# Two exchanges in TensorE's order within an attention visit: a q/k turn with the output product, the turn of x with a q/k product

## The chip, the cores and the metric

One core of a Trainium2 chip runs the whole program. The metric is the device time of one execution in microseconds. A kernel is executed several times and the median is given; one further execution is profiled.

## The reference, cut to what matters

Four blocks run one after the other on 16 sequences of 256 tokens with 128 channels. The change is in the last of them, a network of six layers, each an attention and then a feed-forward part:

```python
def attn_layer(x, Wqkv, qs, ksc, Wo):        # 16 heads of 64, x is 256 x 128 per sequence
    q, k, v = jnp.split(x @ Wqkv, 3, -1)
    q = l2norm(q) * qs;  k = l2norm(k) * ksc
    q = q * cos * scale + rotate_half(q) * sin * scale
    k = k * cos / scale + rotate_half(k) * sin / scale
    out = local_attention(q, k, v)           # windows of 32 look at themselves and the one before
    return out @ Wo                          # added to x
```

(Condensed: the reshapes to heads and the shift of half the channels by one token are left out.)

## The kernel before, in words

All activations stay on the chip. In `l1_network` the five engines each have a program of their own, held together by semaphores; each engine works through its program strictly in the written order. A layer has a prologue, 16 attention visits (one for a sequence, written `attention(N, u, b, prev, nxt, nxt2)`, with N the running number of the sequence and u its parity), and the feed-forward part. `prev`, `nxt` and `nxt2` say whether there is a sequence before, after, and two after this one in the layer.

A visit is a software pipeline over two halves j = 0, 1 (128 tokens each). In a half, TensorE works on three sequences: it finishes N - 1 (or the first half of N), scores N, and prepares N + 1. Its program, L2112 to L2169, in the order of a half:

1. masks into the score banks (L2046), then the attention products of the half before, `weigh` (L2083, 128 small matmuls);
2. two q/k products of N + 1 (`project_qk`, L2008) and two v products (L2015); each is one matmul of 128 x 512 that runs in two passes;
3. the scores (L2058, 128 small matmuls);
4. two output turns (`turn_output`, L2031, four transposes of 128 x 128 each), which ScalarE copies (L2285);
5. the output product (`output`, L2038, eight matmuls in two passes each), which VectorE adds to X (L2454);
6. four q/k turns (`turn_qk`, L2024, four transposes each; numbers 4 to 7 of N in half 0, 0 to 3 of N + 1 in half 1), which ScalarE copies (L2279). They read what GpSimd normed (L1927). Between the first and the second stand the turns of the attention weights (`turn_weights`, L2070, eight transposes), between the second and the third a third q/k product;
7. in half 1, if there is a sequence two after, the turn of its x (`turn_x`, L2001, two transposes), which ScalarE copies in two parts (L2253, L2254) for the products of the next visit;
8. the fourth q/k product, whose square ScalarE takes (L2259) before VectorE rotates it (L2410).

The PSUM banks set a second order. The q/k products have banks 0 and 1 in turn. All of v products, output turns, output product ("y"), q/k turns and the turn of x share banks 2 and 3, which alternate in the order of the list `SHARED` (L1660). Each use waits until the use two before it, which had the same bank, has been read:

```python
for use in SHARED:
    if there[use[2]]:
        out[use] = (2 + at % 2, before[-2])
        before.append(use)
        at += 1
```

`freed` (L1985) turns the kind of that earlier use into a wait: for a turn or an output turn it is ScalarE's copy, for y it is VectorE's addition. The order of ScalarE is a list of its own (L2312 to L2349): in each half the squares, the inverse norms, the copies of v, the two copies of output turns, two exponentials, the copy of the first q/k turn, two copies of turned weights, the copy of the second, a square, the copies of the third and fourth, a square; at the end of half 1 the copy of x. VectorE's order in a half (L2419 ff., `attention`) is: the output's norm, two rotations, a sum of squares, the maxima, a sum of squares, the addition of y (L2454), the sums of exponentials (L2436) and their reciprocals, two more rotations.

Of the kernel before, what the change touches and what calls it, by code (L numbers as in the profile page):

```python
# [80 lines left out]
def held(eng, passed):  # L81

    eng.sem_inc(passed, 1)
# [1554 lines left out]
def l1_network(nc, env, weights, consts):  # L1638
# [16 lines left out]
    def place(c):  # L1655

        return c // 4, 1 - c // 2 % 2, c % 2


    SHARED = ([("v", 0, 1), ("v", 1, 1), ("o", 2, -1), ("o", 3, -1), ("y", 0, -1)] + [("turn", 4 + r, 0) for r in range(4)]  # L1660
              + [("v", 2, 1), ("v", 3, 1), ("o", 0, 0), ("o", 1, 0), ("y", 1, -1)]
              + [("turn", r, 1) for r in range(4)] + [("x", 0, 2)])

    def banks(u, prev, nxt, nxt2):

        there = {-1: prev, 0: True, 1: nxt, 2: nxt2}
        before = [("turn", 3, 0), ("x", 0, 1)] if nxt else [("turn", 2, 0), ("turn", 3, 0)]
        at = u if nxt else 0
        out = {}
# [5 lines that stand above are left out]
        if not nxt:  # L1675
            for use in (("y", 0, 0), ("o", 2, 0), ("o", 3, 0), ("y", 1, 0)):
# [3 lines that stand above are left out]
        return out  # L1680
# [7 lines left out]
    with ExitStack() as ctx:  # L1688
# [121 lines left out]
        def after(eng, s, value):  # L1810

            eng.wait_ge(s, value + START)
# [171 lines left out]
        def _(pe):  # L1984
            def freed(kind, c, N):  # L1985

                if kind == "x":
                    after(pe, s_xT, N + 1)
                elif kind == "v":
                    after(pe, s_V, 4 * N + c + 1)  # L1990
                elif kind == "turn":
                    after(pe, s_qkT, 8 * N + c + 1)
                elif kind == "o":
                    after(pe, s_OT, 4 * N + c + 1)
                elif kind == "y":
                    after(pe, s_x, 2 * N + c + 1)
# [7 lines left out]
            def project_qk(N, c):  # L2004
                j, t, half = place(c)
                after(pe, s_t, 8 * N + c - 1)
                after(pe, s_xT, N + 1)
                nc.tensor.matmul(pp[:, c % 2, :], xT[:, j * P:(j + 1) * P],  # L2008
                                 wqkv[:, t * I + 512 * half:t * I + 512 * half + 512],
                                 start=True, stop=True).then_inc(s_qk, 1)  # L2010
# [8 lines left out]
            def turn_qk(N, r, bank):  # L2019
                j, t, half = place(r)  # L2020
                after(pe, s_kn, 8 * N + r + 1)
                for g in range(4):
                    o = 512 * half + g * P
                    last = nc.tensor.transpose(pp[:, bank, g * P:(g + 1) * P], pre[:, j, t, o:o + P], ident[:, :])  # L2024
                last.then_inc(s_turn, 1)
# [9 lines left out]
            def output(N, j, bank):  # L2035
                after(pe, s_OT, 4 * N + 2 * j + 2)
                for k in range(I // P):
                    last = nc.tensor.matmul(pp[:, bank, 0:C], OT[:, j, k % 2, k // 2, :],  # L2038
                                            wo[:, k, :], start=(k == 0), stop=(k == I // P - 1))
                last.then_inc(s_y, 1)  # L2040

            def masks(N, j):

                after(pe, s_sub, 4 * N + 2 * j)
                for e in range(2):
                    nc.tensor.matmul(pS[:, e, :].rearrange("p (i s) -> p i s", s=2 * W), eye[:, :],  # L2046
                                     bcast(win[:, j, :], 1, 8), start=True, stop=False, skip_group_check=True)
# [17 lines left out]
            def turn_weights(N, j):  # L2065
                for e in range(2):
                    after(pe, s_On, 4 * N + 2 * j)
                    after(pe, s_E, 4 * N + 2 * j + e + 1)
                    for c in range(4):
                        last = nc.tensor.transpose(pW[:, e, c * P:(c + 1) * P], E[:, e, c * P:(c + 1) * P],  # L2070
                                                   ident[:, :])
                    last.then_inc(s_ETp, 1)

            def weigh(u, j):
                for c in range(4):
                    for e in range(2):
                        for w in range(NW):
                            m = (NW * j + w) // 2
                            v = V if w % 2 else Vx
                            o = c * P + e * D  # L2080
                            for f in range(2):
                                r = D * f
                                last = nc.tensor.matmul(pW[W * w:W * w + W, f, o:o + D],  # L2083
                                                        ET[r:r + D, e, c, W * w:W * w + W],
                                                        v[r:r + D, u, m, o:o + D], start=True, stop=True)
                                if c == 3 and e == 1 and w == NW - 1:
                                    last.then_inc(s_PV, 1)

            def weights_ready(pair, N, u, j):
                after(pe, s_ET, 4 * N + 2 * j + 2)  # L2090
                if j == 0:
                    after(pe, s_vx[u], 288 * (pair + 1))
# [19 lines left out]
            def attention(N, u, b, prev, nxt, nxt2):  # L2112
                at = banks(u, prev, nxt, nxt2)

                def bank(*use):
                    kind, c, d = at[use][1]
                    freed(kind, c, N + d)
                    return at[use][0]

                for j in range(2):  # L2120
                    if j == 1:
                        weights_ready(pairs[0], N, u, 0)
                    elif prev:
                        weights_ready(pairs[0], N - 1, 1 - u, 1)
                    if not nxt:
                        after(pe, s_qkT, 8 * N + 4 * j + 4)
                    masks(N, j)
                    if j == 1:
                        weigh(u, 0)
                    elif prev:  # L2130
                        weigh(1 - u, 1)
                    if nxt:
                        project_qk(N + 1, 4 * j)
                        project_qk(N + 1, 4 * j + 1)
                        after(pe, s_qkT, 8 * N + 4 * j + 4)
                        project_v(N + 1, 2 * j, bank("v", 2 * j, 1))
                        project_v(N + 1, 2 * j + 1, bank("v", 2 * j + 1, 1))
                    scores(j)
                    if j == 1:
                        turn_output(N, 0, bank("o", 0, 0))  # L2140
                        turn_output(N, 1, bank("o", 1, 0))
                    elif prev:
                        turn_output(N - 1, 2, bank("o", 2, -1))
                        turn_output(N - 1, 3, bank("o", 3, -1))
                    if prev:
                        output(N - 1, j, bank("y", j, -1))
                    d = j
                    if nxt or not d:
                        turn_qk(N + d, 4 - 4 * j, bank("turn", 4 - 4 * j, d))
                    turn_weights(N, j)  # L2150
                    if nxt or not d:
                        turn_qk(N + d, 5 - 4 * j, bank("turn", 5 - 4 * j, d))
                    if nxt:
                        project_qk(N + 1, 4 * j + 2)
                    if nxt or not d:
                        turn_qk(N + d, 6 - 4 * j, bank("turn", 6 - 4 * j, d))
                        turn_qk(N + d, 7 - 4 * j, bank("turn", 7 - 4 * j, d))
                    if j == 1 and nxt2:
                        turn_x(N + 2, u, bank("x", 0, 2))
                    if nxt:  # L2160
                        project_qk(N + 1, 4 * j + 3)
                if not nxt:
                    weights_ready(pairs[0], N, u, 1)
                    held(pe, s_held)
                    weigh(u, 1)
                    output(N, 0, bank("y", 0, 0))
                    turn_output(N, 2, bank("o", 2, 0))
                    turn_output(N, 3, bank("o", 3, 0))
                    output(N, 1, bank("y", 1, 0))  # L2169
# [527 lines left out]
```

## Time and profile before

| | |
|---|---|
| median of 3 runs | 4761.02 us (4757.34 to 4762.45) |
| profiled execution, its own time | 4745.73 us |
| span of its profile, first to last instruction | 4743.8 us |
| TensorE matmuls busy | 4145.6 us (87%) |
| VectorE, ScalarE, GpSimd busy | 3378.1 us (71%), 2449.9 us (52%), 2175.5 us (46%) |
| mean granted clock of TensorE | 0.957 |

The span is what lies between the first and the last instruction of the profiled execution; the 1.9 us around it belong to the same execution. The busy times are sums over the whole program, of which the six layers are the stretch from about 1,100 us on. In the rows, PE is TensorE's matmul, PEld its load of weights, ACT ScalarE, DVE VectorE, POOL GpSimd; `n_pp<-ident,n_pre` is what is written and what is read. A "x8" behind a row is the number of instructions that it merges.

### The profile page before, as it was taken

Reading aid. Unit: us, or ns where it says so; the run is one execution under the profiler, and the core shown is the slowest. Engines: PE = TensorE matmul, PEld = TensorE weight load, DVE = VectorE, ACT = ScalarE, POOL = GpSimd, SP = SyncE. Lnnn points to the kernel's source line nnn. Section 1 sums busy time; section 2 is a strip of 40 time slices with the busy share of each in tenths; the row PEclk is TensorE's granted clock in tenths of the full one; section 3 lists DMA queues with packets and bytes.
Section 4 is the critical chain, followed back from the end, with each engine's and each line's share of the span. In section 5 each row is a group of like instructions: output and inputs, shape, how many; then the busy total and the mean of one; then the engine's idle time right before and its main releaser. Section 6 shows DMA issues by size and latency. Waiting matters only on the chain. (4 is left out here: it accounts for less than half of the span.)

```text
span 4743.8 us, 176625 instructions
## 1 busy us (share of the span) xinstructions
PE 4145.6 (87%) x69298; PEld 2855.8 (60%) x69299; DVE 3378.1 (71%) x7216; ACT 2449.9 (52%) x5482; POOL 2175.5 (46%) x2301
## 2 busy tenths in 40 slices
PE   7999658576999889998899988999889998999985
PEld 4666426454666556665566655666556665566663
DVE  4777441676888678886788867888678886788866
ACT  4666323124666446664466644666446664466642
POOL 2444200104666246663466634666336664366641
PEclk9999779898999999999999999999999999999998
DMA  1000003003333123331233322233213332133321
GB/s 40 6 5 2 1 24 94 7 0 96 69 70 66 41 57 67 65 68 45 49 69 69 64 51 49 64 66 70 54 40 69 69 69 55 40 66 66 69 44 36
DMA packets 453897, 243.33 MB, mean 51 GB/s; under 512 B 41158, under 2 KB 447892, under 8 KB 452116
## 3 DMA queue, kind: packets, MB, share of 16 engines
q1 hardware_dynamic: 453140, 232.66, 22.0%
q8 instruction: 545, 8.93, 0.8%
q14 instruction: 212, 1.74, 0.1%
HBM read 35.40 MB, written 4.19 MB: 8 GB/s over the span
## 5 line engine op out<-in xcount | busy, mean ns | idle before, releaser
L1913 POOL TENSOR_TENSOR n_pre<-n_tt 128x512 f32<-128x512 f32 x768 | 970.9, 1275 | 894.0 <-DVE n_tt L2410 894.0
L2410 DVE TENSOR_TENSOR n_tt<-n_pp,n_rot 128x1024 f32<-128x1024 f32 x768 | 922.4, 1221 | 378.8 <-ACT n_sq L2259 378.8
L1927 POOL TENSOR_TENSOR n_pre<-n_pre,n_rn 128x512 f32<-128x512 f32 x768 | 776.7, 1042 | 285.0 <-ACT n_rn L2267 285.0
L2008 PE MATMUL n_pp<-n_wqkv,n_xT 128*128 128x512 f32 x1536 | 785.8, 613 | 10.9 <-ACT n_xT L2254 10.5
L2259 ACT ACTIVATE n_sq<-n_pp 128x512 f32<-128x512 f32 x768 | 458.7, 597 | 593.7 <-PE n_pp L2008 583.3
L2417 DVE TENSOR_REDUCE n_ss<-n_sq 128x8 f32<-128x512 f32 x768 | 519.2, 676 | 0.0
L2279 ACT COPY n_qkT<-n_pp 128x512 f32<-128x512 f32 x768 | 436.6, 594 | 136.4 <-PE n_pp L2024 136.0
L2024 PE MATMUL n_pp<-ident,n_pre 128*128 128x128 f32 x3072 | 434.2, 274 | 19.7 <-POOL n_pre L1927 14.6
L2038 PE MATMUL n_pp<-n_wo,n_OT 128*128 128x128 f32 x3072 | 396.9, 282 | 57.1 <-ACT n_OT L2285 57.1
L2024 PEld LDWEIGHTS n_pp<-ident,n_pre 128*128 128x128 f32 x3072 | 361.1, 142 | 129.9 <-issue 126.2
L2038 PEld LDWEIGHTS n_pp<-n_wo,n_OT 128*128 128x128 f32 x3072 | 359.8, 192 | 102.5 <-ACT n_OT L2285 101.2
L2285 ACT COPY n_OT<-n_pp 128x512 f32<-128x512 f32 x384 | 207.1, 589 | 337.2 <-PE n_pp L2031 337.1
L2015 PE MATMUL n_pp<-n_wqkv,n_xT 128*128 128x512 f32 x768 | 366.0, 596 | 0.0
L2058 PEld LDWEIGHTS n_pS<-n_qkT 64*32 64x32 f32 x24576 | 254.6, 105 | 162.3 <-issue 162.3
L301 POOL TENSOR_TENSOR a_E<-a_E,a_ri 128x256 f32<-128x256 f32 (+1 forms) x256 | 211.4, 826 | 291.7 <-DVE a_ri L536 291.1
L2008 PEld LDWEIGHTS n_pp<-n_wqkv,n_xT 128*128 128x128 f32 x1536 | 249.5, 192 | 138.0 <-issue 109.6
L2083 PE MATMUL n_pW<-n_V,n_ET 64*32 64x64 f32 x12288 | 296.2, 225 | 28.8 <-issue 28.6
L2424 DVE TENSOR_REDUCE n_nm<-n_pS 128x8 f32<-128x512 f32 x384 | 247.5, 686 | 98.9 <-PE n_pS L2058 98.9
L2083 PEld LDWEIGHTS n_pW<-n_Vx,n_ET 64*32 64x32 f32 x12288 | 250.1, 105 | 107.3 <-issue 107.3
L2058 PE MATMUL n_pS<-n_qkT 64*32 64x64 f32 (+1 forms) x24576 | 288.1, 222 | 23.5 <-issue 23.5
L2083 PE MATMUL n_pW<-n_Vx,n_ET 64*32 64x64 f32 x12288 | 290.6, 225 | 15.7 <-issue 10.7
L2447 DVE TENSOR_TENSOR n_On<-n_pW,n_ri 128x512 f32<-128x512 f32 x384 | 246.3, 683 | 65.7 <-PE n_pW L2083 63.9
(251 smaller groups left out, 7217.3 us busy)
## 6 DMA issues: line engine op xcount, KB each, us to landing
n_V<-n_Vn SPq DMA_DIRECT2D x768, 128.0 KB, 2.6
n_Vx<-n_Vn SPq DMA_DIRECT2D x384, 128.0 KB, 2.5
n_Vx<-n_Vn SPq DMA_DIRECT2D x576, 64.0 KB, 2.2
n_wqkv<-in_L_ffn_Wqkv SPq DMA_DIRECT2D x6, 1536.0 KB, 6.8
e_w<-in_L_ffn_w SPq DMA_DIRECT2D x32, 256.0 KB, 3.0
m_Y<-e_ye SPq DMA_DIRECT2D x64, 64.0 KB, 2.1
n_wo<-in_L_ffn_Wo SPq DMA_DIRECT2D x6, 512.0 KB, 7.2
a_xs<-in_L_attn_x SPq DMA_DIRECT2D x16, 128.0 KB, 2.1
```

Of the source, the lines that this page charges most:

```text
L1913: nc.gpsimd.tensor_tensor(d, s[0], s[1][:, :, ::-1, :], ALU.add).then_inc(s_add, 1)
L1927: nc.gpsimd.tensor_tensor(d, d, bcast(rn[:, j, t, 8 * half:8 * half + 8], 2, D), ALU.mult).then_inc(s_kn, 1)
L2008: nc.tensor.matmul(pp[:, c % 2, :], xT[:, j * P:(j + 1) * P], wqkv[:, t * I + 512 * half:t * I + 512 * half + 512], start=True, stop=True) ...
L2015: nc.tensor.matmul(pp[:, bank, :], xT[:, j * P:(j + 1) * P], wqkv[:, 2 * I + 512 * half:2 * I + 512 * half + 512], start=True, stop=True). ...
L2024: last = nc.tensor.transpose(pp[:, bank, g * P:(g + 1) * P], pre[:, j, t, o:o + P], ident[:, :])
L2038: last = nc.tensor.matmul(pp[:, bank, 0:C], OT[:, j, k % 2, k // 2, :], wo[:, k, :], start=(k == 0), stop=(k == I // P - 1))
L2058: last = nc.tensor.matmul(pS[W * w:W * w + W, e, i * 2 * W + o:(i + 1) * 2 * W], qkT[r:r + D, 0, i, q:q + W], qkT[r:r + D, 1, i, lo:q + W] ...
L2083: last = nc.tensor.matmul(pW[W * w:W * w + W, f, o:o + D], ET[r:r + D, e, c, W * w:W * w + W], v[r:r + D, u, m, o:o + D], start=True, stop ...
L2259: nc.scalar.activation(sq[:, c % 2, :], pp[:, c % 2, :], ACT.Square).then_inc(s_sq, 1)
L2279: nc.scalar.copy(qkT[:, t, 4 * half:4 * half + 4, j * P:(j + 1) * P], pp[:, bank, :].rearrange("p (g q) -> p g q", g=4)).then_inc(s_qkT, 1)
L2410: nc.vector.tensor_tensor(tt[:, c % 4, :, :].rearrange("p s (h d) -> p s h d", d=D), bcast(pp[:, c % 2, :].rearrange("p (h d) -> p h d", d ...
L2417: nc.vector.tensor_reduce(ss[:, j, t, 8 * half:8 * half + 8], sq[:, c % 2, :].rearrange("p (h d) -> p h d", d=D), AX.X, ALU.add).then_inc( ...
```

## The change

Only TensorE's order and the list of bank uses change; all other engines keep their programs. In both halves the first of the four q/k turns goes ahead of the output product, behind the output turns. In half 1 the turn of x goes behind the fourth q/k product. `SHARED` is rewritten to the new order, so the alternation of banks 2 and 3 and the waits that follow from it change with it.

```diff
-    SHARED = ([("v", 0, 1), ("v", 1, 1), ("o", 2, -1), ("o", 3, -1), ("y", 0, -1)] + [("turn", 4 + r, 0) for r in range(4)]
-              + [("v", 2, 1), ("v", 3, 1), ("o", 0, 0), ("o", 1, 0), ("y", 1, -1)]
-              + [("turn", r, 1) for r in range(4)] + [("x", 0, 2)])
+    SHARED = ([("v", 0, 1), ("v", 1, 1), ("o", 2, -1), ("o", 3, -1), ("turn", 4, 0), ("y", 0, -1)]
+              + [("turn", r, 0) for r in range(5, 8)]
+              + [("v", 2, 1), ("v", 3, 1), ("o", 0, 0), ("o", 1, 0), ("turn", 0, 1), ("y", 1, -1)]
+              + [("turn", r, 1) for r in range(1, 4)] + [("x", 0, 2)])
...
-                    if prev:
-                        output(N - 1, j, bank("y", j, -1))
                     d = j
                     if nxt or not d:
                         turn_qk(N + d, 4 - 4 * j, bank("turn", 4 - 4 * j, d))
+                    if prev:
+                        output(N - 1, j, bank("y", j, -1))
                     turn_weights(N, j)
...
+                    if nxt:
+                        project_qk(N + 1, 4 * j + 3)
                     if j == 1 and nxt2:
                         turn_x(N + 2, u, bank("x", 0, 2))
-                    if nxt:
-                        project_qk(N + 1, 4 * j + 3)
```

## Rows read from the trace of the kernel before

**Rows 1.** The page: the span, and TensorE's granted clock in 40 slices.
```profile
span 4743.8 us, 176625 instructions
...
PEclk9999779898999999999999999999999999999998
```

**Rows 2.** Windows, with x, without: length, busy PE, PEld, DVE, ACT, POOL, clock, DMA, GB/s.
```profile
2589.81:2605.22 15.41, 14.74 (x322) 10.38 (x321) 12.49 (x20) 9.78 (x20) 9.63 (x11) 1.00 0.31 68
2605.22:2619.82 14.60, 14.30 (x320) 10.17 (x319) 12.41 (x20) 9.16 (x18) 9.34 (x10) 1.00 0.32 67
```

**Rows 3.** Timeline of TensorE's matmuls, same stretch: start, us, what, idle before, releaser.
```profile
2591.98 1.04 PE L2024 MATMUL n_pp<-ident,n_pre 128*128 128x128 f32 x8
2593.39 0.43 PE L2001 MATMUL n_pp<-ident,n_xs 128*128 128x128 f32 x2 [0.37 <-ACT n_qkT L2279]
2593.66 1.05 PE L2008 MATMUL n_pp<-n_wqkv,n_xT 128*128 128x512 f32 x2
2594.54 0.59 PE L2046 MATMUL n_pS<-n_win,n_eye 128*128 128x512 bf16 x2
...
2596.48 1.98 PE L2008 MATMUL n_pp<-n_wqkv,n_xT 128*128 128x512 f32 x4
...
2601.51 1.09 PE L2031 MATMUL n_pp<-ident,n_On 128*128 128x128 f32 x8
2602.90 2.05 PE L2038 MATMUL n_pp<-n_wo,n_OT 128*128 128x128 f32 x16 [0.29 <-ACT n_OT L2285]
2604.78 0.60 PE L2024 MATMUL n_pp<-ident,n_pre 128*128 128x128 f32 x4
...
2607.39 1.04 PE L2024 MATMUL n_pp<-ident,n_pre 128*128 128x128 f32 x8
2608.26 1.02 PE L2008 MATMUL n_pp<-n_wqkv,n_xT 128*128 128x512 f32 x2
2609.13 0.59 PE L2046 MATMUL n_pS<-n_win,n_eye 128*128 128x512 bf16 x2
```

**Rows 4.** Table of waits, whole span: total us, how many, longest.
```profile
PE n_pp L2038 <- ACT n_OT L2285: 57.1, 183, 0.8
...
PE n_pW L2083 <- issue: 39.3, 64, 1.2
...
PE n_pp L2001 <- ACT n_qkT L2279: 31.1, 84, 0.4
```

**Rows 5.** Timeline of ScalarE in the same stretch.
```profile
2592.68 1.07 ACT L2279 COPY n_qkT<-n_pp 128x512 f32<-128x512 f32 x2
2594.74 0.60 ACT L2259 ACTIVATE n_sq<-n_pp 128x512 f32<-128x512 f32 x1 [1.00 <-PE n_pp L2008]
...
2595.60 0.37 ACT L2254 COPY n_xT<-n_pp 64x256 f32<-64x256 f32 x1
...
2602.26 1.07 ACT L2285 COPY n_OT<-n_pp 128x512 f32<-128x512 f32 x2 [1.45 <-PE n_pp L2031]
...
2605.48 0.59 ACT L2279 COPY n_qkT<-n_pp 128x512 f32<-128x512 f32 x1 [0.68 <-PE n_pp L2024]
```

**Rows 6.** Timeline of TensorE in a layer's first visit.
```profile
2341.38 1.09 PE L2031 MATMUL n_pp<-ident,n_On 128*128 128x128 f32 x8
2342.77 0.66 PE L2024 MATMUL n_pp<-ident,n_pre 128*128 128x128 f32 x4 [0.30 <-ACT n_OT L2285]
```

**Rows 7.** Timelines of GpSimd and VectorE, same stretch as rows 3.
```profile
2599.62 4.04 POOL L1927 TENSOR_TENSOR n_pre<-n_pre,n_rn 128x512 f32<-128x512 f32 x4 [1.08 <-ACT n_rn L2267]
...
2604.99 0.29 DVE L2454 TENSOR_TENSOR X<-n_pp,X 128x128 f32<-128x128 f32 x1 [0.27 <-PE n_pp L2038]
...
2608.22 1.23 DVE L2410 TENSOR_TENSOR n_tt<-n_pp,n_rot 128x1024 f32<-128x1024 f32 x1 [1.48 <-ACT n_sq L2259]
```

**Rows 8.** Timeline of TensorE inside the small attention products.
```profile
2627.70 0.21 PE L2083 MATMUL n_pW<-n_Vx,n_ET 64*32 64x64 f32 x1 [1.18 <-issue]
```

**Rows 9.** Window in a layer's prologue, columns as in rows 2.
```profile
2301.98:2307.24 5.26, 5.25 (x7) 2.14 (x8) 3.30 (x5) 1.19 (x2) 1.24 (x1) 0.50 0.28 59
```

## The prediction

> **What bounds the kernel now.** I began with the page. The span is 4743.8 us, and the line of granted clock is at 9 in every slice from the eleventh (1186 us) on but the last, which covers the six layers nearly whole [rows 1]. The change touches only the attention visits of these layers, so the next view was the busy time of each engine over two neighbouring halves of visits [rows 2]. In the half that turns x, TensorE is busy 14.74 of 15.41 us, in the half that does not, 14.30 of 14.60. VectorE has 12.4 to 12.5, ScalarE 9.2 to 9.8, GpSimd 9.3 to 9.6. TensorE bounds the stage. It works strictly in the written order, so what it waits for in the visit is time of the kernel, until another engine comes close; VectorE has 2 us of room in each half.
>
> The timeline of TensorE [rows 3] then shows where it stands still. Reading starts of instructions (their ends overlap), eight turns in a row take 0.87 us when nothing interrupts them (2607.39 to 2608.26), so 0.109 each. In the half with x, the same eight turns begin at 2591.98 and the turn of x at 2593.39: 1.41 instead of 0.87, a hole of 0.54. The other hole stands between the eight output turns and the output product: 2601.51 to 2602.90, 1.39 instead of 0.87, a hole of 0.52. The table of waits names the same two on the matmul side and counts them: 84 waits before the turn of x for the copy of a q/k turn, 183 before the output product for a copy of the output turns [rows 4]. Its sums (31.1 and 57.1 us) are lower than 84 x 0.54 and 183 x 0.52, because it begins each wait at the modelled end of the matmul before.
>
> **The turn of x behind the last q/k product.** Nothing is added: one product (two passes) and two turns change places. The turn of x takes the bank of turn 2, so it cannot start before ScalarE has copied that out. The two copies (turns 2 and 3) start at 2592.68 and take 1.07 together [rows 5]; one alone takes 0.59, so the first ends at 2593.27, and the turn of x starts 0.12 later. The product needs none of this: its bank is 1, its x is long there, and it asks only for an earlier rotation. After the change it starts where turn 3 ends, at 2591.98 + 0.87 = 2592.85, and by the other half takes 0.87 to its successor (2608.26 to 2609.13). The turn of x may then start at 2593.72, 0.33 after its bank is free. So the hole closes fully.
>
> What is it worth? From the first of the eight turns to the masks takes 2594.54 - 2591.98 = 2.56 us now, against 2609.13 - 2607.39 = 1.74 in the half without x; two turns of x add 0.22, which makes 1.96 and a saving of 0.60. The hole alone is 0.54. The difference of 0.06 may belong to the two short turns themselves, and stay. I take 0.57. It happens 84 times (14 visits in each of 6 layers): **48 us**, with 45 and 50 as ends.
>
> What could be late next? The first product of the next visit needs the copy of x. Now the copy's second part starts at 2595.60 and ends at 2595.97, and the product starts at 2596.48 [rows 3, 5]. The product would now come at 2595.91. But the copy stands on ScalarE behind the square of the last q/k product, and that square starts 1.08 after its product (2593.66 to 2594.74), so at 2593.94; the copies follow at 2594.4 and 2594.8 and end at 2595.2. The copy of x gets earlier by 0.8, more than the 0.57 by which it is needed earlier. No DMA is moved past any queue, and SyncE's and GpSimd's instruction orders stay.
>
> **The first q/k turn ahead of the output product.** Four turns (0.437 us) go ahead of sixteen passes (1.89 us). The obvious reading is that they fill the hole of 0.52. The bank rule says otherwise: banks 2 and 3 alternate, and each use waits for the use two before it to be copied. The output product waits now for the copy of the first output turn, since that has its bank. After the change the q/k turn has that place and that wait, and the product inherits the wait for the second copy. There is a row for exactly this order: in the first visit of a layer there is no output product, and the q/k turn follows the output turns directly. It starts at 2342.77 after output turns at 2341.38 [rows 6]: 1.39 us, the hole unchanged.
>
> So the q/k turn starts at 2602.90 and is issued by 2603.33. The two copies start at 2602.26 and end together at 2603.33 [rows 5]. As the product now follows the end of the first copy (2602.85) by 0.05, it will start at 2603.38: **0.04 us later** than the same sum without a wait. The ends are 0, if the wait is hidden, and 0.11, the interval of one turn, if the weights have to be loaded anew behind the wait. It applies to 29 halves of each layer (the last half has no q/k turn), 174 in all: a loss of **7 us**, ends 0 and 19.
>
> Is the data there? The first q/k turn reads what GpSimd normed. The four norms start at 2599.62 and take 4.04 [rows 7], so the first ends near 2600.6, 2.3 us ahead of its new place. What is late next: the product ends 0.48 later, so VectorE's addition of it (2604.99, already after 0.27 idle) starts at about 2605.47 and pushes the sums and the reciprocal behind it. That chain has 1.48 us of idle time ahead of the next rotation [rows 7], so 1.0 is left. Turn 5 now waits for the copy of turn 4 in place of that addition. ScalarE makes that copy at 2605.48 now [rows 5], and earlier after the change, since the turn is ready before the exponentials end. Turn 5 is due after four turns and eight weight turns, at 2604.78 + 12 x 0.109 = 2606.09, so nothing waits there.
>
> **Sum.** -48 + 7 = -41 us against the profiled execution's own time of 4745.73 (span 4743.8 and 1.9 around it), which gives 4704.7. The median shown is 4761.02, 0.3% above this execution; I carry the same difference over: **4720 us**. Ends: -50 + 0 and -45 + 19, so 4711 to 4735, and some 4 us each way for the spread of the runs.
>
> **Rivals.**
> *The code arrives too late.* TensorE sometimes stands inside the small attention products with nothing that the profile shows to wait for: 1.18 us idle in one place [rows 8]. I read this as waiting for its own instructions, since 128 small products take only 1.3 us. If the closed hole is what let the fetch keep up, the stall grows by what was saved: at most 84 x 0.57 = 48 us back, so 4761 to 4768. For it: the hole lies just ahead of the masks and these products. Against it: of 192 halves with such products only 64 places show a wait of this kind, 39.3 us in all [rows 4], and the hole is there in 84. 7%. The Trainium skill (Runtime: NRT & Kernel Launch, Instruction fetch mechanics) holds that fetching is hidden behind the rate of issue. By that rule this rival has no chance and the sum stays 4720; the row with 1.18 us speaks against the rule here.
>
> *The q/k turn does fill the hole*, the banks notwithstanding: 174 x 0.44 = 77 us more, 4643. Against it stands the row of the first visit. 3%.
>
> *The product's new wait costs more*, 0.2 to 0.25 each, by a second emptying of TensorE's pipeline: the loss is 35 to 44 us, and the result 4748 to 4757, still just faster or the same. For it: two stops in a row, in place of one. 6%.
>
> *VectorE becomes the bound, and the kernel slower.* The mechanism is the addition of y, 0.48 later, in front of the sums, the reciprocal and the rotation. It decides if the idle time before the rotation is not spare, that is, if less than 0.48 of the 1.48 can be used. Then each of 174 halves grows by 0.48, 84 us, less the 48: 4797. Against it: the rotation waits for a square that waits for TensorE, and so moves with TensorE. 5%.
>
> *The clock falls.* Twelve turns with a stop between them stand in a row after the change. In a prologue, a window of 5.26 us holds six passes of projections and touches a seventh, at 0.50 granted [rows 9]: 0.88 a pass, against 0.43 at full clock (0.87 for two [rows 3]). If the stretch of 3.7 us from output turns to weight turns ran at half clock in each of the 174 halves, the cost would be up to 640 us. Against it: the half with x has ten turns in a row with a stop among them now, and is granted 1.00 [rows 2]. 2%. The Trainium skill (TensorE: Matmul & The Clock Gate, Part 4: PE-mode transpose) says that turns do not count as activity for the clock, a rule against this change; the granted 1.00 in a stage with 66 turns a visit (32 of q and k, 16 of weights, 16 of the output, 2 of x) is what this trace has to set against it.
>
> **How the numbers follow.** My forecast, hole of x closed and the other kept, has 77%. With the three rivals on the faster side or near it, faster has 0.77 + 0.03 + half of the 6% = 0.83; within 0.2% (9.5 us, about what a measurement of this kernel can tell from no change) has the code rival and the other half, 0.10; slower has VectorE and the clock, 0.07. The range of 4703 to 4745 is the forecast's ends, the spread, and part of the third rival.
>
> **What would show each step.** In the changed kernel: from the eight turns to the last q/k product 0.87 us in both kinds of half, no wait before the turn of x, the half with x at 14.8 to 14.9 us instead of 15.41; the wait for a copy of the output turns now at the q/k turn with the old 0.52, and a small one, of some hundredths, at the output product; the addition on VectorE with 0.7 idle ahead of it and the rotation still waiting for the square. I am wrong if the stalls in the small products grow, if the turn of x still waits, or if the output product's own wait is over 0.1.

## The result, and the profile after

The changed kernel takes 4717.62 us (median of 4 runs, 4707.97 to 4719.15) against 4759.18 of the kernel before in the same comparison: ratio 0.9908, 95% interval 0.9891 to 0.9925, which is 36 to 52 us less. The forecast was 4720, 41 us less than before. The two profiled executions differ by less, 4719.15 - 4745.73 = -26.6 us: the one of before happened to be 13 us below this median, and that of after is 1.5 above. Below, lengths of stretches inside the visits are compared, where this scatter is small. One execution of a later experiment, e4_code_shifted, took 6254.51 us at a granted clock of 0.614 (the others 0.949 and more); it is left out of that kernel's median and ratio.

The page of the changed kernel, to be read beside [rows 1]:

```profile
span 4717.2 us, 176625 instructions
...
PE 4144.5 (88%) x69298; PEld 2862.0 (61%) x69299; DVE 3376.9 (72%) x7216; ACT 2447.1 (52%) x5482; POOL 2176.5 (46%) x2301
...
PEclk9999779798999999999999999999999999999998
```

The line of the clock kept its 9 in the layers. The windows from weight turns to weight turns, with x and without (columns as in [rows 2]):

```profile
2578.32:2593.23 14.91, 14.73 (x323) 10.37 (x322) 12.50 (x18) 9.82 (x20) 9.70 (x11) 1.00 0.31 67
2593.23:2607.87 14.64, 14.35 (x320) 10.14 (x319) 12.41 (x18) 9.14 (x18) 9.26 (x10) 1.00 0.34 72
```

The half with x went from 15.41 to 14.91 us; the half without is 14.64 (14.60 before). The timeline of TensorE beside [rows 3]:

```profile
2575.94 0.66 PE L2025 MATMUL n_pp<-ident,n_pre 128*128 128x128 f32 x4 [0.29 <-ACT n_OT L2286]
2576.43 2.05 PE L2039 MATMUL n_pp<-n_wo,n_OT 128*128 128x128 f32 x16
2578.32 1.04 PE L2071 MATMUL n_pW<-ident,n_E 128*128 128x128 f32 x8
...
2580.49 1.04 PE L2025 MATMUL n_pp<-ident,n_pre 128*128 128x128 f32 x8
2581.36 1.02 PE L2009 MATMUL n_pp<-n_wqkv,n_xT 128*128 128x512 f32 x2
2582.22 0.38 PE L2002 MATMUL n_pp<-ident,n_xs 128*128 128x128 f32 x2
2582.44 0.59 PE L2047 MATMUL n_pS<-n_win,n_eye 128*128 128x512 bf16 x2
...
2584.38 1.98 PE L2009 MATMUL n_pp<-n_wqkv,n_xT 128*128 128x512 f32 x4
```

From the eight turns to the masks it is now 2582.44 - 2580.49 = 1.95 us, where 2.56 stood. The turn of x has no idle time before it. The q/k turn (L2025, the L2024 of before) now stands behind the output turns with the same 0.29 of idle, and the output product starts 0.49 behind it instead of 0.44. ScalarE around the turn of x, and VectorE behind the output product, beside [rows 5] and [rows 7]:

```profile
2582.42 0.60 ACT L2260 ACTIVATE n_sq<-n_pp 128x512 f32<-128x512 f32 x1 [0.17 <-PE n_pp L2009]
...
2583.28 0.37 ACT L2255 COPY n_xT<-n_pp 64x256 f32<-64x256 f32 x1
```

```profile
2593.43 0.29 DVE L2455 TENSOR_TENSOR X<-n_pp,X 128x128 f32<-128x128 f32 x1 [0.81 <-PE n_pp L2039]
...
2596.23 1.22 DVE L2411 TENSOR_TENSOR n_tt<-n_pp,n_rot 128x1024 f32<-128x1024 f32 x1 [1.03 <-ACT n_sq L2260]
```

The copy of x ends at 2583.65, 0.73 us ahead of the product that needs it; the addition of y has 0.81 of idle before it (0.27 before), and the rotation 1.03 (1.48 before). The table of waits, beside [rows 4]:

```profile
PE n_pp L2025 <- ACT n_OT L2286: 52.7, 180, 0.3
...
PE n_pW L2084 <- issue: 49.7, 64, 1.6
```

The 84 waits before the turn of x are gone. The other hole has changed its owner. And one row has grown that should have stayed: standing time in the small attention products, 39.3 us before, 49.7 now.

### The profile page after: what moved, and what is told of

Same layout as the page of the kernel before. It is cut to its first block and busy times, and to the rows that moved or that the text cites. A ratio compares the mean times of both kernels' runs of the same rounds, so it can differ in the third digit from the quotient of the medians.

```text
span 4717.2 us, 176625 instructions
## 1 busy us (share of the span) xinstructions
PE 4144.5 (88%) x69298; PEld 2862.0 (61%) x69299; DVE 3376.9 (72%) x7216; ACT 2447.1 (52%) x5482; POOL 2176.5 (46%) x2301
## 3 DMA queue, kind: packets, MB, share of 16 engines
q8 instruction: 545, 8.93, 0.8%
q14 instruction: 212, 1.74, 0.1%
## 5 line engine op out<-in xcount | busy, mean ns | idle before, releaser
L2025 PE MATMUL n_pp<-ident,n_pre 128*128 128x128 f32 x3072 | 445.1, 278 | 70.0 <-ACT n_OT L2286 52.7
L2025 PEld LDWEIGHTS n_pp<-ident,n_pre 128*128 128x128 f32 x3072 | 353.2, 142 | 221.8 <-issue 126.0
```

## The experiments

Three questions were open: which part made what, what the growth of the last row is, and whether the hole that stayed can be closed. Where a kernel is set against the changed one, it goes over the two ratios to the kernel before, and by the medians only where that is said, since not all comparisons ran on the same chip.

### The two parts alone

**e1_x_only** is the kernel before with the lower half of the diff alone:

```diff
-                    if j == 1 and nxt2:
-                        turn_x(N + 2, u, bank("x", 0, 2))
                     if nxt:
                         project_qk(N + 1, 4 * j + 3)
+                    if j == 1 and nxt2:
+                        turn_x(N + 2, u, bank("x", 0, 2))
```

> The turn of x behind the last q/k product, and nothing else of the change. If the change is the sum of its parts, this part alone is worth more than the whole: 84 holes of 0.57 to 0.61 us, so 48 to 52 us less than before, and some 10 us less than the changed kernel. The code rival says that closing the holes makes TensorE's standing times inside the small attention products (idle, released by issue) longer by about 10 us, which leaves 38 to 42 us; by my forecast's reading they stay at the 39.3 us of the kernel before. The half with x is 14.80 to 14.85 us long instead of 15.41.

Measured: 4713.96 us, ratio 0.9907 (0.9883 to 0.9930), which is 33 to 56 us less, 44 in the middle. The table of waits:

```profile
PE n_pp L2038 <- ACT n_OT L2285: 55.9, 180, 0.8
...
PE n_pW L2083 <- issue: 52.1, 62, 1.6
```

The whole gain of the change comes from this part. The row of the small products rises by 12.8 us, to 52.1: the code rival had it at about 10, my forecast at nothing, so some 13 of the 51 us go back here. The time alone cannot tell 44 from the 48 to 52 of the forecast or from the rival's 38 to 42; the row can.

**e2_turn_only** is the changed kernel with the turn of x and the last q/k product in their old order:

```diff
-                    if nxt:
-                        project_qk(N + 1, 4 * j + 3)
                     if j == 1 and nxt2:
                         turn_x(N + 2, u, bank("x", 0, 2))
+                    if nxt:
+                        project_qk(N + 1, 4 * j + 3)
```

> The first q/k turn ahead of the output product, and nothing else. My theory: no gain, since the q/k turn inherits the bank wait of 0.52 and the product gets a second one; 174 times 0.04 to 0.06 us, so 7 to 11 us slower than before. Rival: the turn fills the hole, 77 us faster. Second rival: the order of turns and product matters for VectorE, which adds y 0.48 later; then the kernel is slower by up to 84 us, and the idle time ahead of the rotation is gone. The wait before the turn of x stays at 84.

Measured: 4760.37 us, ratio 1.0012 (1.0000 to 1.0024): 0 to 11 us slower, 6 in the middle. Timeline of TensorE, and two rows of its table of waits:

```profile
2501.84 1.09 PE L2032 MATMUL n_pp<-ident,n_On 128*128 128x128 f32 x8
2503.23 0.66 PE L2025 MATMUL n_pp<-ident,n_pre 128*128 128x128 f32 x4 [0.29 <-ACT n_OT L2286]
2503.72 2.05 PE L2039 MATMUL n_pp<-n_wo,n_OT 128*128 128x128 f32 x16
2505.60 1.04 PE L2071 MATMUL n_pW<-ident,n_E 128*128 128x128 f32 x8
```

```profile
PE n_pW L2084 <- issue: 40.4, 66, 1.1
...
PE n_pp L2002 <- ACT n_qkT L2280: 31.0, 84, 0.4
```

The q/k turn starts 1.39 us after the output turns, as the output product did, and the product 0.49 after it, where four turns alone take 0.437. So the hole is kept and 0.05 to 0.06 added; over all 174 halves the mean from q/k turn to product is 0.492 us (85.6 us in total, from the starts in the trace), where 174 times four turns are 76.0: 9.6 us. In the changed kernel it is 0.493, or 9.7 us. The turn does not fill the hole, and VectorE is not the bound: both rivals fall. The row of the small products stays at 40.4, so it is the other part that makes it grow.

### What the standing time in the small products is

In these calls (`weigh`, 128 products, 1.27 us undisturbed) TensorE stands still with nothing that the profile shows to wait for. The same stop in the fourth layer, before and after:

```profile
3044.02 0.30 PE L2083 MATMUL n_pW<-n_V,n_ET 64*32 64x64 f32 x3 [0.61 <-issue]
```

```profile
3030.33 0.30 PE L2084 MATMUL n_pW<-n_V,n_ET 64*32 64x64 f32 x3 [1.05 <-issue]
```

Each layer runs the same code in a loop, so the stops can be compared by the number of the call within a layer (0 to 31). I took every distance of over 0.25 us between successive starts inside a call, and its mean over those of the six layers that have one:

| call | 0 | 2 | 4 | 7 | 9 | 14 | 16 | 19 | 21 | 26 | all, us |
|---|---|---|---|---|---|---|---|---|---|---|---|
| before | 0.85 | 0.88 | 0.63 | 0.88 | 0.84 | 0.70 | 0.78 | 0.89 | 0.95 | 1.04 | 53.8 |
| changed | 0.99 | 0.87 | 0.80 | 1.50 | 1.11 | 0.89 | 0.58 | 1.39 | 1.29 | 0.97 | 64.8 |
| e1_x_only | 0.78 | 0.98 | 0.72 | 1.43 | 1.41 | 0.91 | 0.69 | 1.25 | 1.47 | 1.06 | 66.4 |
| e2_turn_only | 0.73 | 0.64 | 0.66 | 1.04 | 1.11 | 0.68 | 0.77 | 1.09 | 0.65 | 0.97 | 56.3 |
| e3_product_in_hole | 1.65 | 1.59 | 1.58 | 1.29 | 0.98 | 1.47 | 1.41 | 1.09 | 1.47 | 1.39 | 85.3 |

(The last column has also the small stops of call 28 and of each layer's last visit.) The stops sit in the same calls and at the same product from layer to layer; now and then a layer has none in one of the calls (in the changed kernel once in calls 0 and 16, twice in call 21). After the change, those of the odd calls grew by 0.27 to 0.62 us where they occur, those of the even calls by 0.19 at most, and call 28 has a stop that it had not (0.57). The odd calls are the ones behind the turn of x. The two parts alone separate this: with the holes of x closed and nothing else (e1_x_only) the four odd calls grew by 0.36 to 0.57, the others by 0.21 at most. With the holes of x open (e2_turn_only) calls 7, 9 and 19 grew too, by 0.16 to 0.27, but call 21 lost 0.30; the sum is 56.3 against 53.8, and call 28 has its new stop, so that one comes with the q/k turn. So a stop grows where the hole just ahead of it was closed. Two runs test whether it is the code that is late.

**e4_code_shifted** is the changed kernel with

```diff
-            pe.wait_ge(s_clear, 3)
+            for _ in range(128):
+                pe.wait_ge(s_clear, 3)
             pe.wait_ge(s_cast, 2)
```

> The changed kernel with 128 waits, each long fulfilled, once ahead of TensorE's program of the layers: they only shift its code, at the cost of a few us once. If TensorE's standing times inside the small attention products are waits for the next block of instructions, these times change their places within a layer (other visits, or other products of the same call), and their sum may change by 10 us or more either way. If they are waits for data or for the banks, they stay where they are, to the visit.

Measured: 4714.56 us (median of five), ratio 0.9926 (0.9900 to 0.9952). By the time it cannot be told from the changed kernel. The 128 waits are 63 instructions in the trace. A stop of the fourth layer, and the row of the table of waits:

```profile
2988.64 0.24 PE L2084 MATMUL n_pW<-n_Vx,n_ET 64*32 64x64 f32 x1 [0.92 <-issue]
...
PE n_pW L2084 <- issue: 36.9, 41, 2.0
```

The stops are now in calls 5, 10, 12, 17, 22, 24 and 29 (1.36, 0.77, 0.86, 1.39, 0.77, 0.79 and 1.74 us in the mean of the layers), and in none of the ten of before. Seven stops have moved by three calls, those of calls 0, 4 and 16 are gone, and the row fell from 49.7 to 36.9.

**e5_code_shifted_a_block** has `range(512)` in the same place.

> The changed kernel with 512 fulfilled waits once ahead of TensorE's program; the 128 of e4_code_shifted showed as 63 instructions, so these are some 256, which at 64 bytes each is one of the 16 KB packets of TensorE's instruction queue. If the standing times in the small products are waits for the next packet, they are back in the places of the changed kernel (in a layer's calls of these products 0, 2, 4, 7, 9, 14, 16, 19, 21, 26, counted from 0, where the shift of 64 had them in 5, 10, 12, 17, 22, 24, 29), and the table of waits gives about 50 us again. If the first shift changed them for another reason, a shift four times as long puts them somewhere else again.

Measured: 4733.1 us, ratio 0.9966 (0.9953 to 0.9979). The same stop as above, and the table of waits:

```profile
3040.69 0.30 PE L2084 MATMUL n_pW<-n_V,n_ET 64*32 64x64 f32 x3 [1.59 <-issue]
...
PE n_pp L2002 <- issue: 47.6, 5, 39.2
...
PE n_pW L2084 <- issue: 46.6, 60, 1.6
```

The 512 waits are 255 instructions in the trace. The stops are back in calls 0, 2, 4, 7, 9, 14, 16, 19, 21 and 26 (and 28), 62.1 us by the count of the table above. A shift of a quarter block moves them, a shift of a whole block brings them back: they are waits for code, tied to blocks of some 256 instructions.

The traces show it directly as well. The page has a queue of instruction packets of 16 KB each (`q8 instruction: 545, 8.93, 0.8%`: packets, MB, share), in the layers one every 6.5 to 6.7 us in the mean. Every one of the 597 stops of over 0.25 us in these products, in all ten kernels, ends 2.1 to 3.3 us after the start of such a packet, and 1.1 to 1.7 us after its end; by chance, fewer than one in five would fall into the 1.2 us of the first of these windows. Between the start of the packet and the stop TensorE begins 224 instructions before the change, 206 after it and 185 in e7_both_holes below (medians), fewer as the stops grow.

The time is above the changed kernel by some 15 us by the medians and 28 by the ratios. The waits have to be passed once, which is 16 to 18 of it: the longest wait before the first turn of x is 39.2 us against 21.1, and that turn starts at 1119.5 instead of 1103.7. The rest is not explained.

The Trainium skill (Runtime: NRT & Kernel Launch, Instruction fetch mechanics) states blocks of 16 KiB, 256 instructions; the two shifts agree. It also holds fetching to be hidden behind the rate of issue; here the 36.9 to 49.7 us of idle time in these kernels say otherwise, in the calls that use up 256 loads and products within 1.3 us.

### The hole that stayed

**e3_product_in_hole** puts a product that needs neither of banks 2 and 3 behind the output turns, in half 0:

```diff
                     d = j
+                    if nxt and j == 0:
+                        project_qk(N + 1, 2)
                     if nxt or not d:
                         turn_qk(N + d, 4 - 4 * j, bank("turn", 4 - 4 * j, d))
...
                     if nxt:
-                        project_qk(N + 1, 4 * j + 2)
+                        project_qk(N + 1, 3 if j == 0 else 6)
...
-                    if nxt:
-                        project_qk(N + 1, 4 * j + 3)
+                    if nxt and j == 1:
+                        project_qk(N + 1, 7)
```

> The changed kernel, and in half 0 of each visit the third q/k product goes into the hole behind the output turns, and the fourth takes its old place. The q/k products have banks 0 and 1 and wait for no copy of banks 2 and 3. My theory: 0.87 us of work covers the whole hole of 0.52 and the second wait of 0.05, in 90 halves of the layers (84 to 90 with output turns): 45 to 50 us less than the changed kernel, about 4670. Rival: turn 7, which waits for the copy of turn 5, comes too early now, with the product no longer where it was, and stands for the time saved: then no change. Second rival: VectorE is the bound by now; then the gain is under 20 us and TensorE waits for a rotation before a q/k product.

Measured: 4676.2 us, ratio 0.9838 (0.9813 to 0.9863); against 0.9908 that is 33 us less than the changed kernel, by the medians 41; both are less than the 45 to 50 that I expected. The timeline of a half 0, and the table of waits:

```profile
2563.95 1.07 PE L2032 MATMUL n_pp<-ident,n_On 128*128 128x128 f32 x8
2564.86 1.02 PE L2009 MATMUL n_pp<-n_wqkv,n_xT 128*128 128x512 f32 x2
2565.72 0.60 PE L2025 MATMUL n_pp<-ident,n_pre 128*128 128x128 f32 x4
2566.15 1.95 PE L2039 MATMUL n_pp<-n_wo,n_OT 128*128 128x128 f32 x16
```

```profile
PE n_pW L2084 <- issue: 70.7, 62, 1.7
...
PE n_pp L2025 <- ACT n_OT L2288: 28.2, 96, 0.3
...
PE n_pW L2071 <- ACT n_E L2293: 11.8, 12, 1.3
```

Output turns, product, q/k turn and output product follow each other without idle time. The number of waits for a copy of the output turns falls from 180 to 96, the wait before the weight turns in first visits from 17.4 to 11.8 us. And the price is there again, which my expectation had left out: 70.7 us in the small products, 21 more than in the changed kernel. In the table above it is the even calls that grew this time, from 0.58 to 0.99 us up to 1.39 to 1.65, and they are the ones behind half 0. Turn 7 is not in the way (the q/k turns wait for a copy of their own kind 6 times, 2.5 us in all, as in the changed kernel) and VectorE is not the bound (a q/k product waits for a rotation twice, 0.5 us).

**e6_hole_and_shift** is that kernel with the 128 waits.

> e3_product_in_hole with its code shifted by the 128 waits. In the changed kernel this shift brought the standing time in the small products from 49.7 to 36.9 us. My theory: these waits grew to 70.7 us in e3_product_in_hole because it moves work away from in front of them, and the shift takes a part back: 15 to 25 us less there, so 4650 to 4665. Rival: the sum depends on the holes closed and not on the place of the packets' ends; then it stays at about 70 and the time at 4676.

Measured: 4666.94 us, ratio 0.9846 (0.9819 to 0.9873). The row:

```profile
PE n_pW L2084 <- issue: 55.7, 42, 1.7
```

The row falls by 15 us, as expected, but the time does not show it: it is just above the expected 4650 to 4665, and its ratio is no lower than that of e3_product_in_hole. The passing of the 128 waits may cost some 4 us (a quarter of the 16 to 18 for 512, an estimate); the rest is within the interval. Inconclusive for the time.

**e7_both_holes** fills both halves. In half 1 the last product has to stand before the last q/k turn, and ScalarE's order follows:

```diff
-                    if nxt and j == 0:
-                        project_qk(N + 1, 2)
+                    if nxt:
+                        project_qk(N + 1, 4 * j + 2)
...
-                    if nxt:
-                        project_qk(N + 1, 3 if j == 0 else 6)
+                    if nxt and j == 0:
+                        project_qk(N + 1, 3)
                     if nxt or not d:
                         turn_qk(N + d, 6 - 4 * j, bank("turn", 6 - 4 * j, d))
-                        turn_qk(N + d, 7 - 4 * j, bank("turn", 7 - 4 * j, d))
                     if nxt and j == 1:
                         project_qk(N + 1, 7)
+                    if nxt or not d:
+                        turn_qk(N + d, 7 - 4 * j, bank("turn", 7 - 4 * j, d))
...
-                    if nxt:
-                        square(N + 1, 4 * j + 2)
+                    if nxt and j == 0:
+                        square(N + 1, 2)
                     if nxt or not j:
                         copy_qk(N + j, 6 - 4 * j, bank("turn", 6 - 4 * j, j))
+                    if nxt and j == 1:
+                        square(N + 1, 6)
+                    if nxt or not j:
                         copy_qk(N + j, 7 - 4 * j, bank("turn", 7 - 4 * j, j))
```

> Both halves get the third q/k product behind the output turns, and in half 1 the fourth stands ahead of the last q/k turn, so that the turn of x has the last q/k turn between itself and the copy it waits for; ScalarE squares the third product of half 1 behind the copy of turn 2. My theory: 84 more holes of 0.5 are closed, but the turn of x waits for 0.1 to 0.3 again, and the standing times in the small products take a part back: 20 to 35 us less than e3_product_in_hole, about 4650. Rival: VectorE is near its bound by now, rotates later, and TensorE waits for it before a q/k product: no gain over e3_product_in_hole.

Measured: 4641.96 us, ratio 0.9775 (0.9757 to 0.9793), 34 us less than e3_product_in_hole by the medians, 30 by the ratios, as expected (20 to 35). Half 1:

```profile
2573.77 1.09 PE L2032 MATMUL n_pp<-ident,n_On 128*128 128x128 f32 x8
2574.70 1.02 PE L2009 MATMUL n_pp<-n_wqkv,n_xT 128*128 128x512 f32 x2
2575.56 0.60 PE L2025 MATMUL n_pp<-ident,n_pre 128*128 128x128 f32 x4
...
2579.53 1.02 PE L2009 MATMUL n_pp<-n_wqkv,n_xT 128*128 128x512 f32 x2
2580.39 0.60 PE L2025 MATMUL n_pp<-ident,n_pre 128*128 128x128 f32 x4
2580.83 0.38 PE L2002 MATMUL n_pp<-ident,n_xs 128*128 128x128 f32 x2
2581.05 0.59 PE L2047 MATMUL n_pS<-n_win,n_eye 128*128 128x512 bf16 x2
```

```profile
PE n_pW L2084 <- issue: 78.6, 61, 1.7
```

In this half no idle time is left between the output turns and the masks, not even before the turn of x, where I had expected 0.1 to 0.3. The small products take 78.6 us.

**e8_both_and_shift** adds the 128 waits.

> e7_both_holes with its code shifted by the 128 waits. By the reading of e4_code_shifted 10 to 20 us less than e7_both_holes, from the table of waits' row on the small products alone; if VectorE is the bound in e7_both_holes, no difference.

Measured: 4633.91 us, ratio 0.9755 (0.9740 to 0.9769).

```profile
PE n_pW L2084 <- issue: 54.6, 42, 1.7
```

The row is lower by 24 us, the median by 8 where I expected 10 to 20, and the intervals of the two ratios overlap. All five executions (4627.33 to 4635.49 us) lie below all five of e7_both_holes (4638.14 to 4654.36) in the same comparison, and the attention stages of the two profiled executions are 20 us apart, so a gain is likely; its size is not shown. This is the fastest kernel of the study, 2.45% below the kernel before and 1.5% below the changed one.

## Why the prediction was right, point by point

**The bound.** TensorE's holes were time of the kernel. The longest step shows it best, from the kernel before to e7_both_holes: 84 holes of x gave 0.61 each (measured in the changed kernel), and 174 behind the output turns shrank from 0.52 to 0.06, together 131 us. The stops in the small products took 40 back (53.8 us to 93.7 by the count of the table), which leaves 91. The attention stages of the two profiled executions, from the first turn of x to the feed-forward part of each layer, are 98 us apart (3057.6 and 2959.2), and the ratio says 98 to 115. Single steps fit less closely: by the same account, with the waits of first and last visits, e3_product_in_hole should be 28 us below the changed kernel in these stages and is 41, e7_both_holes 34 below that and is 29. Part of this is scatter: e5_code_shifted_a_block runs the changed kernel's code in the layers, and its stages are 8.6 us shorter (3020.4 against 3029.0).

**The turn of x.** The mechanism was as told: the hole closed, the copy of x came earlier than its need (0.73 us of room, 0.71 by the prediction's times), and the difference from turns to masks was 1.95 us where the working had 1.96. But I then took 0.57 for a saving of 0.60, with 50 us as the upper end. It is 0.61, and 84 of it is 51 us. The term that was too small is the hedge: "may belong to the two short turns themselves, and stay". The comparison with the other half had already given the right number. The half with x is 14.91 us long, at the edge of the 14.8 to 14.9 forecast.

**The q/k turn.** The wait went over to it (0.52, and 180 waits in the table), and the output product got a second one. The term was 0.04 a time and 7 us; it measured 0.056 and 9.7. "The row of the first visit" forecast this order truly. e2_turn_only confirms the sign, at the edge of its interval.

**What had been costed at nothing.** The code rival had 7% as a thing that takes all or nothing. It took a part: 10 us of the 51 in the changed kernel, 13 in e1_x_only. The prediction's own sign, "I am wrong if the stalls in the small products grow", came true, so its mechanism was incomplete although its time was right. "Against it: of 192 halves ... only 64 places show a wait of this kind" read the row wrongly: the places were fixed, four of the ten per layer lay right behind a hole that was closed, and the stops there grew by 0.3 to 0.6 us. It belonged in the sum as a term, with 0 and 48 as ends.

**The sum.** By terms the change is -51 + 10 + 11 = -30 us, and that is what the attention stages of the two profiled executions differ by, 3057.6 and 3029.0 us, 28.6 apart. The medians differ by 41.6, with an interval from 36 to 52. So the forecast of 41 met the measured number with three terms that were off by 3, 3 and 11, and the account by rows ends some 6 us short of the interval. That it came within 1 us is in part luck: with the code term at its measured size it would have said 30. In e1_x_only the term is 51 - 13 = 38 and the middle 44, but there 38 lies within the interval. What the 6 to 12 us are stays open. The profiled execution of before is itself faster than all four others of its kernel in that comparison, the stages of one and the same code differ by 8.6 us between two executions, and the stops in the small products vary between the layers of one execution, in the changed kernel from 8.2 to 13.2 us a layer.

**The other rivals.** VectorE had 1.03 us of idle time left before the rotation, against 1.0 forecast, and never became the bound, not even at 4634 us (there q/k products wait 0.7 us in all for a rotation). The clock kept 1.00 in the halves with twelve turns and a stop. The rule of the Trainium skill on turns (TensorE: Matmul & The Clock Gate, Part 4: PE-mode transpose) spoke against the change; nothing here shows the effect.

## What to carry to other kernels

Where buffers rotate, as banks 2 and 3 do here, moving work within the rotation moves the wait along with it; work that uses none of them fills the hole (0.87 us of q/k product did, four turns did not). Look for a place in the trace of before where the new order already exists. And before closing a hole, see what stands right behind it: a burst of small instructions may be living on that pause, and a part of the gain goes there (8 to 21 us a step here).

## What the runs showed of the hardware that I had not expected

TensorE waits for its own code in bursts of small products, although the code runs straight on within a layer. The stops keep their places from layer to layer, move by three calls or vanish when 63 instructions are put ahead, and return when four times as many are. Each ends 2.1 to 3.3 us after the start of a 16 KB packet of instructions. They grew from 39.3 us to 78.6 as the pauses between the bursts were closed, and fell to 54.6 by a shift that costs one line. Why a closed pause makes the stop longer by half of the pause and more (0.27 to 0.62 for 0.54 to 0.61) was not tried by itself and is open.
